# Top-32 attention: the masks of the kept keys come from ScalarE's Sign instead of a VectorE compare, and their count from row sums

## The chip, the core and the metric

The kernel runs on one core of one Trainium2 chip. The metric is the device time of one launch in microseconds. A core has TensorE (PE) for matmuls and transposes, VectorE (DVE), ScalarE (ACT), GpSimd (POOL), and SyncE (SP), which here issues most DMAs. Each engine works through a queue of its own in order, and semaphores tie the queues together.

## The reference, cut to what matters

A model of four residual blocks over x of 4 batches x 512 rows x 256: a 16-head cross-attention, a top-2 mixture of eight experts, the block below, and a 16-head self-attention with gated values. The change touches only the attention in the third block:

```python
Q = (x_text @ Wq).reshape(Bb, Tt, H, DH)            # 4 heads of 32
K = (x_vision @ Wk).reshape(Bb, Gg, H, DH)          # 1601 keys
scores = jnp.einsum('bthd,bghd->bhtg', Q, K) / np.sqrt(DH)
scores = jnp.where(vision_mask[:, None, None, :], scores, -jnp.inf)
topv, topi = jax.lax.top_k(scores, 32)
probs = jax.nn.softmax(topv, axis=-1)
attn = jnp.zeros_like(scores).at[bi, hi, ti, topi].set(probs)
attn_mean = attn.mean(axis=1)                       # over the heads
c_t = jnp.einsum('btg,bgd->btd', attn_mean, x_vision @ Wv)
```

So each query row keeps exactly the 32 largest of its 1601 scores, takes a softmax over those, and the heads' sparse rows are averaged.

## The kernel before, in words

The program runs the first block for all four batches, then the experts, then, batch by batch, the third and the fourth block. In the third, the top-32 attention of a batch is cut into 16 items: item n is tile t = n // 4 of 128 query rows and head h = n % 4. An item is a matrix of 128 rows by 1601 keys. The order of the work is written out by hand in each engine's queue; nothing is planned by a tool. Semaphore counts are per batch, which is what the helper `nth` adds.

The steps of item n and their lines:

- PE, `scores(n)` (L1483 to L1491): four column groups into PSUM banks 0 to 3, each a matmul of queries and keys (L1489) and one of the mask row (L1490). It waits until ScalarE has evicted the scores of n-1, as there is one set of banks.
- ScalarE, `score_out(n)` (L1013): evicts 1601 columns to one of four buffers in SBUF.
- VectorE, `search(n, k)` (L2239): the eight largest of each of 27 parts of 60 columns, as 216 candidates. It is spread over the steps of item n-1. Then four maxima (L2254) and three replacements (L2256) over the 216 give the 32 largest candidates.
- VectorE: the negated maximum (L2265, `top_ready`), then the mask `kept01`: 1 where the score is at least the 32nd candidate (L2269, `choice_ready`), in bf16, double buffered.
- ScalarE: Exp of the whole row (L1048), Exp of the 32 with their sum (L1051).
- PE, `count(n)` (L1493 to L1502): 13 matmuls of a column of ones with the mask, which leave column counts; ScalarE copies these with a row sum into one number (L1050, `count_ready`).
- VectorE, `settle(n-1)` (L2200 to L2219), in the middle of item n: reads that number. If it is not 128 x 32, some row had more than 32 kept (nine of its 32 in one part, or a tie), and an exact search over 1601 columns is run. Then `weight` (L2221 to L2227) takes one over the sum (`w1_ready`).
- GpSimd: multiplies probabilities and mask (L802), and later adds the head to the mean of its tile (L796). ScalarE scales in between (`scale_head`, L1033). The last two heads of a batch are multiplied and added by VectorE (L2278, L2281).
- PE: once per tile, transposes of the mean (L1511) and two blocks of 26 matmuls with the values (L1519, `context`), interleaved with the items; ScalarE evicts the transposes (`attn_turned`, L834 and L830) and the result (L1017).

PE's queue in the loop (L1529 to L1543) is: scores(n+2); for n % 4 = 2 from 6 on 12 transposes; for n % 4 = 0 from 8 on a context block; count(n); for n % 4 = 3 from 7 on a context block; for n % 4 = 2 a wait for the count's copy and the 13th transpose. ScalarE's (L1041 to L1058) is: eviction of n+2, Exp(n), the count's copy, the small Exp, scaling of n-1, and for n % 4 = 2 the evictions of the transposes.

Of the kernel before, what the change touches and what calls it, by code (L numbers as in the profile page):

```python
# [8 lines left out]
BF16 = mybir.dt.bfloat16  # L9
# [6 lines left out]
P = 128  # L16
# [21 lines left out]
H1, D1, TOPK = 4, 32, 32  # L38
ALL_DECIDED = int(np.float32(P * TOPK).view(np.int32))
DROPPED = -3.4e38  # L40
# [28 lines left out]
def program(nc, a, dbg=None):  # L69
    ctx = ExitStack()  # L70
    with ctx:
        def sb(name, shape, dt=F32):
            return ctx.enter_context(nc.sbuf_tensor("sb_" + name, shape, dt))
# [56 lines left out]
        ones_row = sb("ones_row", [1, P], BF16)  # L130
        ones_col = sb("ones_col", [P, 1], BF16)
        norms = sb("norms", [P, 4])
# [108 lines left out]
        kept01 = at(o, [2, KS], BF16); o += KS  # L241
        kept_by_col = at(o, [P]); o += P
        probs1 = at(o, [3, KS]); o += 3 * KS
# [200 lines left out]
        sum1_ready = sem("sum1_ready", 16)  # L444
        choice_ready = sem("choice_ready", 16)
        count_ready = sem("count_ready", 16)
# [249 lines left out]
        def _(pool):  # L696
# [79 lines left out]
            for b in range(NBATCH):  # L776
# [21 lines left out]
                for n in range(TILES * H1 - 2):  # L798
                    e = probs1[:, n % 3, 0:GKEYS]
                    pool.wait_ge(e1_ready, nth(b, e1_ready, n + 1))  # L800
                    pool.wait_ge(w1_ready, nth(b, w1_ready, n + 1))
                    G.tensor_tensor(e, e, kept01[:, n % 2, 0:GKEYS], ALU.mult).then_inc(p1_kept, 1)  # L802
                    if n >= 1:
                        add_head(n - 1)
# [33 lines left out]
        def _(act):  # L838
# [154 lines left out]
            for b in range(NBATCH):  # L993
# [32 lines left out]
                def scale_head(n):  # L1026
                    t = n // H1
                    act.wait_ge(p1_kept, nth(b, p1_kept, n + 1))
                    act.wait_ge(w1_ready, nth(b, w1_ready, n + 1))
                    if n % H1 == 0 and t >= 2:  # L1030
                        act.wait_ge(aT_done, nth(b, aT_done, 4 * (t - 1)))
                    p = probs1[:, n % 3, 0:GKEYS]
                    A(p if n % H1 else p_mean[:, t % 2, 0:GKEYS], p, ACT.Copy, scale=stat1[:, n % 3, WEIGHT:WEIGHT + 1]).then_inc(p1_scaled, 1)  # L1033

# [6 lines left out]
                for n in range(TILES * H1):  # L1041
# [3 lines left out]
                    if n >= 3:  # L1045
                        probs_used(n - 3)
                    bias = stat1[:, n % 3, NEG:NEG + 1]
                    A(probs1[:, n % 3, 0:GKEYS], s_sb[n % 4][:, 0:GKEYS], ACT.Exp, bias=bias).then_inc(e1_ready, 1)  # L1048
                    act.wait_ge(count_done, nth(b, count_done, n + 1))
                    A(kept_by_col[0:1, :], ps[0:1, 7, 3 * P:4 * P], ACT.Copy, accum_out=kept[0:1, n:n + 1]).then_inc(count_ready, 1)  # L1050
                    A(top_e[:, n % 2, :], top[:, n % 2, :], ACT.Exp, bias=bias,  # L1051
                      accum_out=stat1[:, n % 3, SUM:SUM + 1]).then_inc(sum1_ready, 1)
                    if 1 <= n < TILES * H1 - 1:
                        scale_head(n - 1)
# [55 lines left out]
        def _(pe):  # L1110
# [344 lines left out]
            for b in range(NBATCH):  # L1455
# [37 lines left out]
                def count(n):  # L1493

                    pe.wait_ge(choice_ready, nth(b, choice_ready, n + 1))
                    if n >= 1:
                        pe.wait_ge(count_ready, nth(b, count_ready, n))
                    for i in range(KCH):
                        k = -i % KCH
                        ins = mm(ps[0:1, 7, 3 * P:3 * P + KW[k]], ones_col[:, :], kept01[:, n % 2, k * P:k * P + KW[k]],  # L1500
                                 start=(i == 0), stop=(i == KCH - 1))
                    ins.then_inc(count_done, 1)  # L1502
# [171 lines left out]
        def _(dve):  # L1674
# [4 lines left out]
            def setup_program():  # L1679
# [16 lines left out]
                link(V.memset(ones_row[:, :], 1.0))  # L1696
                link(V.memset(ones_col[:, :], 1.0))
                link(V.memset(every[:, :], 1.0))
# [492 lines left out]
            for b in range(NBATCH):  # L2191
# [53 lines left out]
                for n in range(NH):  # L2245
# [17 lines left out]
                    if n >= 3:  # L2263
                        dve.wait_ge(p1_scaled, nth(b, p1_scaled, n - 2))
                    V.tensor_scalar(st[:, NEG:NEG + 1], eights[:, 0:1], -1.0, None, ALU.mult).then_inc(top_ready, 1)  # L2265
                    if n >= 2:
                        dve.wait_ge(p1_kept, nth(b, p1_kept, n - 1))

                    V.tensor_scalar(kept01[:, n % 2, 0:GKEYS], s, eights[:, TOPK - 1:TOPK], None, ALU.is_ge).then_inc(choice_ready, 1)  # L2269

                mean = p_mean[:, (TILES - 1) % 2, 0:GKEYS]
                for n in (NH - 2, NH - 1):
                    if n == NH - 1:
                        settle(n)
                        weight(n)
                    dve.wait_ge(w1_ready, nth(b, w1_ready, n + 1))
                    dve.wait_ge(e1_ready, nth(b, e1_ready, n + 1))
                    link(V.scalar_tensor_tensor(s_cut[:, 0:GKEYS], kept01[:, n % 2, 0:GKEYS], stat1[:, n % 3, WEIGHT:WEIGHT + 1],  # L2278
                                                probs1[:, n % 3, 0:GKEYS], ALU.mult, ALU.mult))
                    dve.wait_ge(p1_added, nth(b, p1_added, n - TILES))  # L2280
                    V.tensor_tensor(mean, mean, s_cut[:, 0:GKEYS], ALU.add).then_inc(p1_added, 1)  # L2281
                dve.wait_ge(p1_added, nth(b, p1_added, TILES * (H1 - 1)))
# [193 lines left out]
```

## Time and profile before

| | us |
|---|---|
| median of 3 runs | 3291.48 |
| lowest and highest | 3287.58, 3298.54 |
| the profiled execution's own time | 3297.39 |
| its span in the profile | 3295.5 |

The span runs from the first to the last instruction of the profiled execution; its own time is that and 1.9 us around it. Granted clock is the share of TensorE's full rate (2.4 GHz) that it was given, in steps of 0.5 and 1; over a stretch it is a mean.

### The profile page before, as it was taken

To read this page: it belongs to the slowest core of one execution; us is meant where nothing else is said; L and a number is where in the kernel's file an instruction comes from. 1 tells how busy PE (TensorE), PEld (TensorE's weight loads), DVE (VectorE), ACT (ScalarE), POOL (GpSimd) and SP (SyncE) were. 2 spreads that over 40 slices of the span, in tenths; PEclk is the share of its full clock that TensorE was granted. 3 is DMA by queue.
4 is the path that set the end of the run, shared out by engine and by line. 5 is a ranking of instruction groups with operands and counts; after the bars stand their busy time and mean duration, and the time that the engine had idled before them with its cause. 6 is when DMAs were issued, how large, how long until landed. Compare 5 with 4: busy or idle time off the path is not lost.

```text
span 3295.5 us, 36665 instructions
## 1 busy us (share of the span) xinstructions
PE 2666.0 (81%) x12668; PEld 1520.5 (46%) x12668; DVE 1837.7 (56%) x4565; ACT 1446.3 (44%) x2310; POOL 1020.1 (31%) x423
## 2 busy tenths in 40 slices
PE   0565889899948996888898878898879798888899
PEld 0522222232225653465574356475356476346467
DVE  8455012121131114865894875795775796685777
ACT  3033567677811222632453541453551354451354
POOL 1023000000011113630751640571460590260292
PEclk9987898999969996889998889998889898789999
DMA  1054842533141111020001011000002000002000
GB/s 55 0 186 156 119 58 53 82 48 44 63 167 41 45 41 39 1 76 25 20 1 39 1 57 43 21 1 14 26 7 93 20 1 7 26 1 93 0 1 7
DMA packets 88476, 146.54 MB, mean 44 GB/s; under 512 B 16724, under 2 KB 58840, under 8 KB 88248
## 3 DMA queue, kind: packets, MB, share of 16 engines
q1 hardware_dynamic: 80760, 134.57, 15.7%
q0 software_dynamic: 7504, 9.35, 1.5%
q8 instruction: 108, 1.77, 0.2%
q14 instruction: 104, 0.85, 0.1%
HBM read 121.17 MB, written 22.88 MB: 44 GB/s over the span
## 4 chain that ended last, share of the span: by engine, by line
PE 61%; DVE 20%; ACT 7%; issue 7%; DMA 3%; SPq 1%; POOL 1%; DVEq 0%; ACTq 0%; POOLq 0%
PE ps L1489 7%; PE ps L1649 6%; PE ps L1640 6%; PE ps L1256 4%; PE ps L1267 4%; PE ps L1519 3%; PE ps L1627 3%; ACT sb_arena L918 3%; PE ps L1424 2%; PE ps L1589 2%; PE ps L1490 2%; DVE sb_arena L2239 2%; PE ps L1443 2%; PE ps L1437 2%; PE ps L1569 2%
## 5 line engine op out<-in xcount | busy, mean ns | idle before, releaser
L918 ACT ACTIVATE sb_arena<-ps 128x1024 f32<-128x1024 f32 x416 | 402.8, 1021 | 177.8 <-PE ps L1256 170.9
L2239 DVE MAX8 sb_arena<-sb_arena 128x8 f32<-128x60 f32 (+1 forms) x1728 | 247.6, 206 | 175.3 <-ACT sb_arena L1013 175.1
L1489 PE MATMUL ps<-sb_arena 128*128 128x512 f32 (+1 forms) x512 | 296.4, 666 | 25.3 <-ACT sb_arena L1013 13.3
L1256 PE MATMUL ps<-sb_arena 96*128 96x512 bf16 x832 | 241.6, 398 | 56.2 <-issue 37.7
L1649 PE MATMUL ps<-sb_arena 128*128 128x512 f32 x512 | 279.4, 630 | 2.7 <-ACT sb_arena L1087 2.7
L688 POOL TENSOR_TENSOR sb_arena<-sb_arena 128x1024 f32<-128x1024 f32 x96 | 223.7, 2330 | 164.8 <-DVEq L2347 153.9
L802 POOL TENSOR_TENSOR sb_arena<-sb_arena 128x1601 f32<-128x1601 f32 x56 | 173.9, 3105 | 314.8 <-DVE sb_arena L2227 314.8
L1640 PE MATMUL ps<-sb_arena 128*128 128x64 f32 x2048 | 260.9, 271 | 0.0
L1640 PEld LDWEIGHTS ps<-sb_arena 128*128 128x128 f32 x2048 | 252.9, 194 | 0.3
L1100 ACT ACTIVATE sb_arena<-ps,sb_arena 128x512 f32<-128x512 f32 x256 | 175.6, 686 | 170.8 <-DVE sb_arena L2388 167.6
L690 POOL TENSOR_TENSOR sb_arena<-sb_arena 128x1024 f32<-128x1024 f32 x84 | 229.9, 2737 | 6.6
L1267 PE MATMUL ps<-sb_arena 128*32 128x512 f32 x1664 | 227.7, 620 | 1.5 <-ACT sb_arena L918 1.5
L2388 DVE TENSOR_REDUCE sb_arena<-ps 128x1 f32<-128x512 f32 x256 | 171.4, 685 | 88.3 <-PE ps L1649 87.8
L737 POOL DMA_INDIRECT taken_rows<-sb_taken,sb_slots x32 | 31.3, 979 | 605.2 <-DVEq L2007 596.6
L1627 PEld LDWEIGHTS ps<-sb_ident,sb_arena 128*128 128x128 f32 x1024 | 130.2, 144 | 189.0 <-issue 125.6
L1013 ACT ACTIVATE sb_arena<-ps 128x1601 f32<-128x1601 f32 x64 | 96.4, 1507 | 248.9 <-PE ps L1490 248.9
L1094 ACT ACTIVATE sb_arena<-ps 128x512 f32<-128x512 f32 x256 | 152.4, 595 | 119.6 <-PE ps L1627 117.1
L1627 PE MATMUL ps<-sb_ident,sb_arena 128*128 128x128 f32 x1024 | 158.3, 278 | 52.4 <-ACT sb_arena L1100 52.4
L1256 PEld LDWEIGHTS ps<-sb_arena 96*128 96x128 bf16 x832 | 58.7, 99 | 271.0 <-ACT sb_arena L918 204.3
L796 POOL TENSOR_TENSOR sb_arena<-sb_arena 128x1601 f32<-128x1601 f32 x40 | 156.6, 3916 | 18.8 <-ACT sb_arena L1033 18.8
L2382 DVE TENSOR_TENSOR sb_arena<-sb_arena,sb_xtn 128x2048 f32<-128x2048 f32 x56 | 149.4, 2667 | 0.1
L1500 PE MATMUL ps<-sb_arena,sb_ones_col 128*1 128x128 bf16 (+1 forms) x832 | 71.8, 253 | 93.7 <-DVE sb_arena L2269 59.8
(343 smaller groups left out, 4798.8 us busy)
## 6 DMA issues: line engine op xcount, KB each, us to landing
sb_arena<-in_ctxT SPq DMA_DIRECT2D x13, 1601.0 KB, 7.4
sb_arena<-k_spill SPq DMA_DIRECT2D x96, 208.0 KB, 8.1
sb_arena<-in_dft SPq DMA_DIRECT2D x5, 2048.0 KB, 7.9
k_spill<-sb_arena SPq DMA_DIRECT2D x12, 832.0 KB, 5.2
sb_arena<-in_w SPq DMA_DIRECT2D x16, 512.0 KB, 6.5
sb_arena<-in_idft SPq DMA_DIRECT2D x4, 2048.0 KB, 9.6
sb_arena<-in_wf SPq DMA_DIRECT2D x8, 1024.0 KB, 13.0
sb_arena<-q_spill SPq DMA_DIRECT2D x96, 64.0 KB, 9.2
```

The source lines that it names most:

```text
L688: link(eng.tensor_tensor(heads(tmp if e else v2[:, :, hs]), src, mix, ALU.mult))
L690: link(eng.tensor_tensor(v2[:, :, hs], v2[:, :, hs], tmp, ALU.add))
L802: G.tensor_tensor(e, e, kept01[:, n % 2, 0:GKEYS], ALU.mult).then_inc(p1_kept, 1)
L918: A(probs0[:, 2 * (m % 4):2 * (m % 4) + 2, :], ps[:, 2 * (m % 2):2 * (m % 2) + 2, :], ACT.Exp).then_inc(pair_probs, 1)
L1100: A(p2[:, n % 4, :], ps[:, S2_BANKS[n % 4], :], ACT.Exp, bias=nmax2[:, t, h:h + 1], accum_out=sums2[:, t, h:h + 1]).then_inc(p2_ready, 1)
L1256: ins = mm(ps[:, 2 * (m % 2) + i, :], k_stack[0:NSPLIT, h, k * P:(k + 1) * P], q_stack[0:NSPLIT, h, :], start=True, stop=True)
L1267: ins = mm(ps[32 * j:32 * j + 32, 4 + q % 2, :], v0s[b % 2][:, k, h * V0W:(h + 1) * V0W], probs0[:, (4 * g + j) % 8, :], start=(k == 0), s ...
L1489: mm(ps[:, j, 0:w], q1z[:, h, t * P:(t + 1) * P], kT1[:, c0:c0 + w], start=True, stop=False)
L1627: ins = tr(ps[:, 2 + n % 2, j * P:(j + 1) * P], p2[:, n % 4, j * P:(j + 1) * P], ident[:, :])
L1640: ins = mm(ps[:, 4 + h % 2, t * D2:(t + 1) * D2], pT2[:, n % 2, j * P:(j + 1) * P], v2[:, j, h * D2:(h + 1) * D2], start=(j == 0), stop=(j ...
L1649: mm(ps[:, S2_BANKS[n % 4], :], q2z[:, h, t * P:(t + 1) * P], kT2[:, h // 2, :], start=True, stop=True).then_inc(s2_done, 1)
L2239: ins = V.max(cand[:, n % 2, 8 * j:8 * j + 8], s_sb[n % 4][:, c0:c0 + w])
```

## The change

The compare L2269 goes. VectorE now makes, beside the negated maximum, a bias per row that is minus the 32nd candidate, moved by 2^-22 of its size so that the candidate itself comes out positive; `top_ready` is raised only behind it. ScalarE takes Sign of score plus bias over the 1601 columns, which gives +1 or -1 in `kept01`, with the row's sum beside it; this is put between the two Exps. PE adds the 128 row sums with one matmul of one column, and ScalarE copies that one number, negated, behind the small Exp. If each row keeps 32, it is 128 x (1601 - 64). Since a dropped key now has -1 where it had 0, the scaling copy becomes Relu, and VectorE's last two products take max(mask, 0) first and the weight in the addition. GpSimd waits for the Sign. `kept01` has two buffers as before; the row sums and the biases have two as well, and ScalarE waits for count and product of n-2 where VectorE waited for the product.

```diff
-ALL_DECIDED = int(np.float32(P * TOPK).view(np.int32))
+ALL_DECIDED = int(np.float32(P * (GKEYS - 2 * TOPK)).view(np.int32))
+JUST_UNDER = 2.0 ** -22
...
-        kept_by_col = at(o, [P]); o += P
+        signs = at(o, [2, 1]); o += 2
+        under = at(o, [2, 2]); o += 4
+        o += P - 6
...
                     pool.wait_ge(e1_ready, nth(b, e1_ready, n + 1))
+                    pool.wait_ge(sign_ready, nth(b, sign_ready, n + 1))
                     pool.wait_ge(w1_ready, nth(b, w1_ready, n + 1))
...
-                    A(p if n % H1 else p_mean[:, t % 2, 0:GKEYS], p, ACT.Copy, scale=stat1[:, n % 3, WEIGHT:WEIGHT + 1]).then_inc(p1_scaled, 1)
+                    A(p if n % H1 else p_mean[:, t % 2, 0:GKEYS], p, ACT.Relu, scale=stat1[:, n % 3, WEIGHT:WEIGHT + 1]).then_inc(p1_scaled, 1)
...
                     A(probs1[:, n % 3, 0:GKEYS], s_sb[n % 4][:, 0:GKEYS], ACT.Exp, bias=bias).then_inc(e1_ready, 1)
-                    act.wait_ge(count_done, nth(b, count_done, n + 1))
-                    A(kept_by_col[0:1, :], ps[0:1, 7, 3 * P:4 * P], ACT.Copy, accum_out=kept[0:1, n:n + 1]).then_inc(count_ready, 1)
+                    if n >= 2:
+                        act.wait_ge(count_done, nth(b, count_done, n - 1))
+                        act.wait_ge(p1_kept, nth(b, p1_kept, n - 1))
+                    A(kept01[:, n % 2, 0:GKEYS], s_sb[n % 4][:, 0:GKEYS], ACT.Sign, bias=under[:, n % 2, 1:2], accum_out=signs[:, n % 2, :]).then_inc(sign_ready, 1)
                     A(top_e[:, n % 2, :], top[:, n % 2, :], ACT.Exp, bias=bias,
                       accum_out=stat1[:, n % 3, SUM:SUM + 1]).then_inc(sum1_ready, 1)
+                    act.wait_ge(count_done, nth(b, count_done, n + 1))
+                    A(kept[0:1, n:n + 1], ps[0:1, 7, 3 * P:3 * P + 1], ACT.Copy, scale=-1.0).then_inc(count_ready, 1)
...
-                    pe.wait_ge(choice_ready, nth(b, choice_ready, n + 1))
+                    pe.wait_ge(sign_ready, nth(b, sign_ready, n + 1))
                     if n >= 1:
                         pe.wait_ge(count_ready, nth(b, count_ready, n))
-                    for i in range(KCH):
-                        k = -i % KCH
-                        ins = mm(ps[0:1, 7, 3 * P:3 * P + KW[k]], ones_col[:, :], kept01[:, n % 2, k * P:k * P + KW[k]],
-                                 start=(i == 0), stop=(i == KCH - 1))
+                    ins = mm(ps[0:1, 7, 3 * P:3 * P + 1], signs[:, n % 2, :], ones[:, :], start=True, stop=True)
                     ins.then_inc(count_done, 1)
...
-                link(V.memset(ones_col[:, :], 1.0))
...
-                    V.tensor_scalar(st[:, NEG:NEG + 1], eights[:, 0:1], -1.0, None, ALU.mult).then_inc(top_ready, 1)
                     if n >= 2:
-                        dve.wait_ge(p1_kept, nth(b, p1_kept, n - 1))
-
-                    V.tensor_scalar(kept01[:, n % 2, 0:GKEYS], s, eights[:, TOPK - 1:TOPK], None, ALU.is_ge).then_inc(choice_ready, 1)
+                        dve.wait_ge(sign_ready, nth(b, sign_ready, n - 1))
+                    low_of, just = under[:, n % 2, 0:1], under[:, n % 2, 1:2]
+                    V.tensor_scalar(st[:, NEG:NEG + 1], eights[:, 0:1], -1.0, None, ALU.mult)
+                    link(V.tensor_scalar(low_of, eights[:, TOPK - 1:TOPK], JUST_UNDER - 1.0, 1.0e-30, ALU.mult, ALU.add))
+                    V.scalar_tensor_tensor(just, eights[:, TOPK - 1:TOPK], -1.0 - JUST_UNDER, low_of, ALU.mult, ALU.max).then_inc(top_ready, 1)
...
-                    link(V.scalar_tensor_tensor(s_cut[:, 0:GKEYS], kept01[:, n % 2, 0:GKEYS], stat1[:, n % 3, WEIGHT:WEIGHT + 1],
-                                                probs1[:, n % 3, 0:GKEYS], ALU.mult, ALU.mult))
+                    link(V.scalar_tensor_tensor(s_cut[:, 0:GKEYS], kept01[:, n % 2, 0:GKEYS], 0.0, probs1[:, n % 3, 0:GKEYS], ALU.max, ALU.mult))
                     dve.wait_ge(p1_added, nth(b, p1_added, n - TILES))
-                    V.tensor_tensor(mean, mean, s_cut[:, 0:GKEYS], ALU.add).then_inc(p1_added, 1)
+                    V.scalar_tensor_tensor(mean, s_cut[:, 0:GKEYS], stat1[:, n % 3, WEIGHT:WEIGHT + 1], mean, ALU.mult, ALU.add).then_inc(p1_added, 1)
```

## Rows read from the trace of the kernel before

**Rows 1.** The page, part 1: busy time, share of the span, instructions

```profile
PE 2666.0 (81%) x12668; PEld 1520.5 (46%) x12668; DVE 1837.7 (56%) x4565; ACT 1446.3 (44%) x2310; POOL 1020.1 (31%) x423
```

**Rows 2.** Busy time by stretch: window, length, PE, PEld, DVE, ACT, POOL, clock, DMA, GB/s

```profile
1297.00:1454.20 157.20, 128.54 (x624) 71.54 (x622) 125.38 (x593) 85.71 (x130) 89.37 (x28) 0.79 0.04 9
```

**Rows 3.** L1013, items 2 to 15, one row per batch: ns, first and last start

```profile
L1013 ACT ACTIVATE sb_arena<-ps x14: 1505/1507/1513, 1297.0 to 1419.3; 128x1601 f32<-128x1601 f32 x14
L1013 ACT ACTIVATE sb_arena<-ps x14: 1505/1507/1513, 1809.1 to 1927.9; 128x1601 f32<-128x1601 f32 x14
L1013 ACT ACTIVATE sb_arena<-ps x14: 1505/1507/1511, 2318.7 to 2437.1; 128x1601 f32<-128x1601 f32 x14
L1013 ACT ACTIVATE sb_arena<-ps x14: 1505/1507/1510, 2836.2 to 2955.1; 128x1601 f32<-128x1601 f32 x14
```

**Rows 4.** Timeline of one period, batch 0: start us, us, engine, line, operation, [idle before]

```profile
1382.09 1.96 DVE L2269 TENSOR_SCALAR sb_arena<-sb_arena 128x1601 bf16<-128x1601 f32 x1
...
1383.03 1.51 ACT L1013 ACTIVATE sb_arena<-ps 128x1601 f32<-128x1601 f32 x1 [2.17 <-PE ps L1490]
...
1384.10 0.86 PE L1500 MATMUL ps<-sb_arena,sb_ones_col 128*1 128x128 bf16 x13 [1.12 <-DVE sb_arena L2269]
1384.43 1.62 ACT L1048 ACTIVATE sb_arena<-sb_arena 128x1601 f32<-128x1601 f32 x1
...
1384.89 1.12 PE L1489 MATMUL ps<-sb_arena 128*128 128x512 f32 x2
1385.95 0.25 ACT L1050 ACTIVATE sb_arena<-ps 1x128 f32<-1x128 f32 x1
...
1386.11 0.18 ACT L1050 ACTIVATION_READ_ACCUMULATOR sb_arena<-ps 1x1 f32 x1
...
1386.50 1.61 ACT L1033 ACTIVATE sb_arena<-sb_arena 128x1601 f32<-128x1601 f32 x1
...
1387.87 0.16 DVE L2225 RECIPROCAL sb_arena<-sb_arena 128x1 f32<-128x1 f32 x1
...
1389.62 1.51 ACT L1013 ACTIVATE sb_arena<-ps 128x1601 f32<-128x1601 f32 x1 [1.50 <-PE ps L1490]
1390.29 0.14 DVE L2265 TENSOR_SCALAR sb_arena<-sb_arena 128x1 f32<-128x1 f32 x1
```

**Rows 5.** Groups by line, 1297 to 1419.3 (batch 0): busy us, mean ns, idle before

```profile
L802 POOL TENSOR_TENSOR sb_arena<-sb_arena 128x1601 f32<-128x1601 f32 x13 | 40.4, 3111 | 79.7 <-DVE sb_arena L2227 79.7
L796 POOL TENSOR_TENSOR sb_arena<-sb_arena 128x1601 f32<-128x1601 f32 x8 | 32.4, 4047 | 0.0
L2269 DVE TENSOR_SCALAR sb_arena<-sb_arena 128x1601 bf16<-128x1601 f32 x13 | 26.7, 2051 | 0.0
...
L1048 ACT ACT_TABLE_LOAD x1 | 1.3, 1283 | 0.0
```

**Rows 6.** Timeline of PE in batch 1, count(1)

```profile
1819.14 1.49 PE L1500 MATMUL ps<-sb_arena,sb_ones_col 128*1 128x128 bf16 x13 [3.80 <-DVE sb_arena L2269]
```

**Rows 7.** Busy time by stretch (columns of rows 2): idle stretch, scores(4), undisturbed scores

```profile
1308.50:1317.00 8.50, 8.50 (x15) 2.50 (x15) 6.59 (x33) 2.19 (x6) 3.02 (x1) 0.50 0.00 0
...
1820.60:1827.40 6.80, 6.80 (x16) 2.04 (x16) 6.57 (x32) 2.19 (x5) 3.02 (x1) 0.67 0.00 0
2325.00:2330.20 5.20, 1.43 (x14) 1.22 (x14) 5.20 (x26) 3.14 (x2) 2.86 (x1) 0.68 0.00 0
2330.20:2338.10 7.90, 7.90 (x15) 2.25 (x15) 6.59 (x33) 2.19 (x5) 3.02 (x1) 0.56 0.01 3
...
1378.37:1383.03 4.66, 4.62 (x12) 1.48 (x12) 4.27 (x25) 2.45 (x7) 2.85 (x1) 1.00 0.00 0
```

**Rows 8.** The chain in order of time, batch 0: start us, us, two context blocks

```profile
1374.48 3.10 PE ps L1519 x26
...
1401.59 4.73 PE ps L1519 x26
```

**Rows 9.** Timeline of VectorE in the tail of batch 0: the weight of item 15

```profile
1440.03 0.21 DVE L2227 TENSOR_SCALAR sb_arena<-sb_arena,sb_tmask 128x1 f32<-128x1 f32 x1
```

More of the change, by code:

```diff
@@ L130, in program @@
         ones_row = sb("ones_row", [1, P], BF16)
-        ones_col = sb("ones_col", [P, 1], BF16)
         norms = sb("norms", [P, 4])
@@ L444, in program @@
         sum1_ready = sem("sum1_ready", 16)
-        choice_ready = sem("choice_ready", 16)
+        sign_ready = sem("sign_ready", 16)
         count_ready = sem("count_ready", 16)
```

## The prediction

> A measurement of this kernel can tell about 0.3% (10 us) from no change.
>
> **What bounds the kernel now.** I read the page first. TensorE is busy 81% of the span, VectorE 56%, ScalarE 44% [rows 1]. That average says little here: the edit touches one stage, the top-32 attention, which runs once in each of four batches. In the first it lasts 157 us, PE works 82% of that at a granted clock of 0.79, VectorE 80% [rows 2]; the other three are alike, so one row stands. So no engine fills the stage; it turns on who waits for whom.
>
> The score eviction (L1013) runs once per item, and its first and last start mark the loop. From that of item 2 to that of item 15 there are 13 periods: 122.3, 118.8, 118.4 and 118.9 us in the four batches, mean 119.6, or 9.2 us a period [rows 3]. These 13 are the ones I have to re-price: in PE's queue the count of item n stands between the scores of item n+2 and those of n+3, for n = 0 to 12.
>
> The timeline of one period shows the order [rows 4]. PE ends its scores, ScalarE evicts them at 1383.03, VectorE ends the compare (L2269, 1382.09 + 1.96 us) at 1384.05, PE starts the 13 count matmuls at 1384.10 and only behind them, at 1384.89, the next scores, which end 4.7 us later: ScalarE evicts again at 1389.62. The compare runs beside the eviction, so PE stood still for only 1.1 us. ScalarE's own work (Exp at 1384.43, two small ones, scaling at 1386.50) lies beside PE's scores and costs nothing. Where VectorE is late, the period is its own: from the compare at 1382.09 to the next L2265 at 1390.29 it is 8.2 us, of which the compare is 2.
>
> **The change, part by part.**
>
> *VectorE loses the compare* (2.05 us a mean of 13 [rows 5]) and gains two one-column operations with one semaphore link; the present one-column L2265 takes 0.14 us [rows 4], so two linked ones are 0.28 at least; I take 0.35. VectorE's loop falls by 1.7 us an item. Whether that arrives depends on the next part.
>
> *ScalarE gains Sign over 1601 columns with a row sum.* It has the shape, source and bias form of the Exp of L1048. Exp's successor starts 1.52 us after it (1384.43 to 1385.95), and the row-sum read that follows the small Copy takes 0.18 [rows 4]; so Sign with its sum is 1.71 us. Bounds: 1.52, and 1.62 + 0.25 = 1.9.
>
> *The wait moves, and this decides.* ScalarE's queue holds the eviction of n+2, Exp(n), Sign(n). PE's holds scores(n+2), count(n), scores(n+3). Count(n) now waits for Sign(n), which stands behind the eviction of scores(n+2). So a closed loop arises: eviction, Exp, Sign, count, next scores, next eviction. Nothing in it overlaps. From eviction to Exp 1.40 us (1383.03 to 1384.43), Exp 1.52, Sign 1.71: 4.63 [rows 4]. The handoff and the one-column matmul in place of 13: the compare-to-count handoff is 0.05, the matmul itself between 0.06 (a thirteenth of the 0.79 us from 1384.10 to 1384.89) and that 0.79, if one costs what the thirteen did; I take 0.15 in all, near the low end, since one column moves in place of 1601. The high end would add 0.7 a period, 36 us in all. Then scores(n+3). PE starts scores 4.8 us after the eviction started, where it was 1.9 in rows 4.
>
> At the full clock scores take 4.7 us, so a plain period is 4.8 + 4.7 = 9.5 us. VectorE is then hidden: from the end of an eviction (1384.54) to L2265 it needs 5.75 us, in which it stands at the count's result after some 2.9 [rows 4]. Now that result comes 4.63 + 0.15 + 0.5 = 5.3 us after the eviction's start, that is 0.9 us late; its loop ends at 1.5 + 5.75 + 0.9 + 0.35 = 8.5 us, and Exp(n+1) is not due before 9.5 + 1.4. The saved compare therefore buys nothing. GpSimd's 3.1 + 4.0 us an item [rows 5] fit in 9.5 as well. ScalarE's sum: 4.63, small Exp and Copy 0.75, scaling 1.6, and in every fourth item the turned probabilities (four evictions of about a third of L1013's 1.51 each, 2.0), together 9.0: hidden. Its new waits for count(n-2) and the product n-2 are for work done a period earlier, and the two waits moved behind Sign are for things ScalarE needs next anyway. GpSimd's added wait for Sign stands ahead of a wait for the weight, which VectorE gives out later: free.
>
> *The clock.* PE's idle stretch grows from 1 or 2 us to 4.6. The trace has a place with just such a stretch: in each batch PE idles 3.8 us before count(1) (batch 1, up to 1819.14 [rows 6]), in the 5.2 us between scores(3) and scores(4). In all four batches the granted clock falls in it (means of 0.68 to 0.80; one of the four rows stands), and scores(4) takes 8.5, 6.8, 7.9 and (batch 3, like the first) 8.5 us at 0.50 to 0.67 instead of 4.66 at 1.00 [rows 7]: 7.9 in the mean, 8.5 when all of it runs at the 1.2 GHz level. A plain period becomes 4.8 + 7.9 = 12.7 us.
>
> *The 13 periods of a batch:*
> - n = 0: 12.7 and a table load of 1.28 [rows 5] that is on the loop now: 14.0.
> - n = 1, 2, 3, 4, 5, 9: plain, 6 x 12.7 = 76.2.
> - n = 6, 10: PE waits for the kept count and turns one last chunk before scores. That count is out at 5.3, the transposes (0.4, for 0.3 and a handoff) at 5.7, so scores start 0.9 later than in a plain one: 2 x 13.6 = 27.2.
> - n = 7, 11: 26 context matmuls stand between count and scores: 3.1 us at full clock, 4.73 where most of it fell in a low stretch [rows 8]. After the idle stretch I take 4.7, and scores behind it at the full clock again, as after the block of rows 8, where the clock had come back: 2 x (4.8 + 4.7 + 4.7) = 28.4.
> - n = 8, 12: the context block (3.1) fills most of the idle stretch, 1.6 us remain: between 9.5 and 12.7, nearer the first as rows 4 kept the clock across 1.1 us; 2 x 10.5 = 21.0.
>
> Sum 166.8 against 119.6: +47.2 a batch, +189 us over four.
>
> *The tail* behind the eviction of item 15: VectorE drops two compares, but Exp(15) and Sign(15) queue on ScalarE behind the turned probabilities of item 14. Today the last weight comes 20.7 us after the eviction (1419.3 [rows 3] to 1440.03 [rows 9]). With the change: top(14) at 7.5, Exp and Sign to 10.8, the small ones to 11.3, scaling and turned chunks to 14.8, Exp(15) and Sign(15) to 18.1, count, copy and weight to 20.0. I take 0. Everything else (Relu for Copy, max for mult in L2278, add in L2281, a memset of one column less at setup) has the same shape as before: 0.
>
> *Tables.* Copy and Exp alternate all through the stage and the trace has one table load there [rows 5]; for Sign no row speaks, bounds 0 and 2 x 1.28 a period. The Trainium skill (ScalarE: Activation LUTs, "Table sets: the hidden batching unit") says cheap functions are in every set as filler, and by that it is 0; no run here shows it yet. The same page ("Rules for kernel authors") sends simple element work to VectorE, up to about three times faster in bf16; by that Sign would be 5.9 us and the sum some 220 us higher, an estimate. The trace disagrees for this shape with an fp32 source: compare 1.96, an activation of 1601 columns 1.62.
>
> The sum stands on the profiled execution, 3297.4 us (span 3295.5), 5.9 above the median 3291.5 and inside the runs shown. Against the median: 3291.5 + 189 = **3480 us**, +5.7%.
>
> **The rivals.**
> 1. *The clock holds.* PE's gaps cost only themselves: 10.8 + 6 x 9.5 + 2 x 10.4 + 2 x 12.6 + 2 x 9.5 = 132.8 a batch, +13.2, +53 in all: 3344. Against it: four falls out of four at an idle stretch shorter than the new one.
> 2. *The clock stays low through the stage:* scores 8.5, context 6.2 (twice 3.1): 14.6 + 6 x 13.3 + 2 x 14.2 + 2 x 19.5 + 2 x 14.9 = 191.6, +72 a batch: 3579. For it: scores(4) was wholly low twice. Against: rows 8 show a context block lifting it again.
> 3. *Faster.* VectorE's loop is the bound in most periods (8.2 us) and its 1.7 us arrive: 13 x 1.7 x 4 = 88, some 5 more in the tail: 3198. This decides as soon as the loop through Sign is shorter than VectorE's; that needs it under 8.2, and it is 9.5 at best, unless scores(n+3) don't stand behind count(n), which the code says they do.
> 4. *Sign needs a table of its own:* 13 x 2.57 x 4 = +134 on top, 3614.
> 5. *The masks miss exactly 32.* The bias is the 32nd value widened by 2^-22 of itself; a neighbour that close sends an item into the exact search (L2206 to L2219), of which the trace has none. Four maxima and four replacements over 1601 columns and two more such passes are some 20 us (ten passes at the compare's 1.96). One or two items: +20 to +40, inside my range; all 64, if Sign is not exact: +1280.
>
> **How the numbers follow.** My forecast, mixed clock, 0.76; rival 1 0.08, rival 2 0.09, rival 3 0.04, rivals 4 and 5 together 0.02; 0.01 that it nets out. The range leaves out rival 1 and the far cases and takes in most of rival 2: 3375 to 3575. Faster 0.04, same 0.01, slower 0.95.
>
> **What would show it.** In the changed profile the chain of waits should alternate ScalarE (eviction, Exp, Sign) and PE (scores) in the stage, and PE's count should wait on Sign in all 64 items. Eviction to eviction should be 9.5 to 13.3 us, first to last some 167 a batch. VectorE should idle at the count's result and be under 65% busy; the stage's clock should be below 0.75. One table load per batch at the Exp. I am wrong if PE starts scores within 3 us of the eviction's start, or if the periods are under 9 us.

## The result, and the profile after

The changed kernel takes 3513.6 us (median of 4, 3512.7 to 3517.3) against 3290.7 for the kernel before on the same chip: ratio 1.068, 95% interval 1.066 to 1.070. It is slower by 6.8%. I had forecast 3480, between 3375 and 3575.

The page of the changed kernel, part 1, and the group of the new count in part 5 (busy us, mean ns, idle before and what ended most of it):

```profile
PE 2709.6 (77%) x11964; PEld 1506.0 (43%) x11964; DVE 1801.1 (51%) x4643; ACT 1541.2 (44%) x2374; POOL 996.8 (28%) x423
...
L1505 PE MATMUL ps<-sb_ones,sb_arena 128*1 128x1 f32 x128 | 12.1, 163 | 295.1 <-ACT sb_arena L1055 227.0
```

VectorE has 37 us less to do than in [rows 1], ScalarE 95 more. PE has 700 instructions fewer and yet is busy for 44 us longer; the granted clock of the whole execution fell from 0.897 to 0.849. And ahead of the count (L1505) PE now stands still for 295 us, 227 of them ended by Sign (L1055).

The eviction's first and last start in each batch, the rows that answer to [rows 3] (L1016 here is L1013 before):

```profile
L1016 ACT ACTIVATE sb_arena<-ps x14: 1505/1507/1509, 1294.9 to 1464.6; 128x1601 f32<-128x1601 f32 x14
L1016 ACT ACTIVATE sb_arena<-ps x14: 1505/1507/1508, 1855.9 to 2027.8; 128x1601 f32<-128x1601 f32 x14
L1016 ACT ACTIVATE sb_arena<-ps x14: 1505/1507/1508, 2424.6 to 2594.4; 128x1601 f32<-128x1601 f32 x14
L1016 ACT ACTIVATE sb_arena<-ps x14: 1505/1507/1511, 2991.2 to 3171.1; 128x1601 f32<-128x1601 f32 x14
```

The 13 periods take 169.7, 171.9, 169.8 and 179.9 us, 691 in all against 478: +213. The tail of a batch, from its last eviction to the first matmul behind its context blocks (L1564, L1560 before), was 35.7 us in the mean of the four and is now 40.0: +17. Everything else together differs by -10 us, in stages that the change does not touch; these take between 2644 and 2675 us in the fourteen profiles of this case, so that -10 says nothing. That makes the 220 us between the two spans.

One plain period of the changed kernel in the timeline, with the steps of [rows 4]:

```profile
1320.44 1.51 ACT L1016 ACTIVATE sb_arena<-ps 128x1601 f32<-128x1601 f32 x1 [4.90 <-PE ps L1497]
1321.84 1.62 ACT L1051 ACTIVATE sb_arena<-sb_arena 128x1601 f32<-128x1601 f32 x1
1323.36 1.62 ACT L1055 ACTIVATE sb_arena<-sb_arena 128x1601 bf16<-128x1601 f32 x1
1324.88 0.19 ACT L1055 ACTIVATION_READ_ACCUMULATOR sb_arena<-sb_arena 128x1 f32 x1
...
1325.12 0.19 PE L1505 MATMUL ps<-sb_ones,sb_arena 128*1 128x1 f32 x2 [4.72 <-ACT sb_arena L1055]
...
1325.24 2.08 PE L1496 MATMUL ps<-sb_arena 128*128 128x512 f32 x2
...
1326.37 0.16 DVE L2228 RECIPROCAL sb_arena<-sb_arena 128x1 f32<-128x1 f32 x1 [1.19 <-ACT sb_arena L1059]
...
1332.92 1.50 ACT L1016 ACTIVATE sb_arena<-ps 128x1601 f32<-128x1601 f32 x1 [5.87 <-PE ps L1497]
```

Read it as one loop: eviction 1320.44, Exp 1.40 later, Sign 1.52 after that, its row sum out at 1325.07, count at 1325.12, scores at 1325.24, next eviction at 1332.92. PE starts scores 4.80 us after the eviction started; the forecast said 4.8. The next scores then took 7.7 us, not 4.7. The reason is in the view of busy time by stretch over the 13 periods of batch 0 (columns as in rows 2):

```profile
1294.90:1464.60 169.70, 116.67 (x312) 49.64 (x312) 92.83 (x546) 89.64 (x115) 69.33 (x22) 0.64 0.01 5
```

The granted clock is 0.64 there; PE is busy 69% of the time, VectorE 55%.

### The profile page after: what moved, and what is told of

It is laid out like the page before. It is cut to its first block, busy times and chain, and to the rows that moved or that the text cites. A ratio compares the mean times of both kernels' runs of the same rounds, so it can differ in the third digit from the quotient of the medians.

```text
span 3515.6 us, 35470 instructions
## 1 busy us (share of the span) xinstructions
PE 2709.6 (77%) x11964; PEld 1506.0 (43%) x11964; DVE 1801.1 (51%) x4643; ACT 1541.2 (44%) x2374; POOL 996.8 (28%) x423
## 4 chain that ended last, share of the span: by engine, by line
PE 60%; DVE 15%; issue 10%; ACT 10%; DMA 2%; SPq 1%; POOL 1%; another core or an unknown queue 1%; DVEq 0%; ACTq 0%; POOLq 0%; PEldq 0%
PE ps L1496 10%; PE ps L1653 6%; PE ps L1644 6%; PE ps L1263 4%; PE ps L1274 4%; PE ps L1631 3%; PE ps L1523 3%; ACT sb_arena L921 3%; PE ps L1497 3%; ACT sb_arena L1055 2%; ACT sb_arena L1051 2%; PE ps L1431 2%; PE ps L1593 2%; PE ps L1450 2%; PE ps L1444 2%
## 5 line engine op out<-in xcount | busy, mean ns | idle before, releaser
L1496 PE MATMUL ps<-sb_arena 128*128 128x512 f32 (+1 forms) x512 | 366.3, 810 | 18.3 <-ACT sb_arena L1008 10.1
L805 POOL TENSOR_TENSOR sb_arena<-sb_arena 128x1601 f32<-128x1601 f32 x56 | 173.8, 3104 | 560.9 <-DVE sb_arena L2230 560.9
L1016 ACT ACTIVATE sb_arena<-ps 128x1601 f32<-128x1601 f32 x64 | 96.4, 1507 | 397.0 <-PE ps L1497 397.0
L1644 PEld LDWEIGHTS ps<-sb_arena 128*128 128x128 f32 x2048 | 252.2, 194 | 0.3
L1505 PE MATMUL ps<-sb_ones,sb_arena 128*1 128x1 f32 x128 | 12.1, 163 | 295.1 <-ACT sb_arena L1055 227.0
L1496 PEld LDWEIGHTS ps<-sb_arena 128*128 128x128 f32 x512 | 109.1, 265 | 95.4 <-issue 67.2
## 6 DMA issues: line engine op xcount, KB each, us to landing
sb_arena<-in_wf SPq DMA_DIRECT2D x8, 1024.0 KB, 13.3
```

Of the source, the lines that this page charges most:

```text
L1496: mm(ps[:, j, 0:w], q1z[:, h, t * P:(t + 1) * P], kT1[:, c0:c0 + w], start=True, stop=False)
L1644: ins = mm(ps[:, 4 + h % 2, t * D2:(t + 1) * D2], pT2[:, n % 2, j * P:(j + 1) * P], v2[:, j, h * D2:(h + 1) * D2], start=(j == 0), stop=(j ...
```

## The experiments

The theory: the loop through ScalarE sets the period (A), PE's longer idle stretch lowers its clock (B). Rivals: ScalarE's added work as such, or the clock alone. Each experiment starts from the changed kernel unless it says otherwise, and its ratio is against the kernel before, run beside it on the same chip. "Less" is against the changed kernel's 3513.6 us, which was measured at another time: the kernel before took 3290.7 us then and between 3279 and 3286 beside the experiments, so a difference of some 12 us in the times alone shows nothing, and there the ratios and the traces decide. A plain period is one with neither transposes nor a context block in it (n = 1 to 5 and 9).

**e1: the count behind the next scores.**

```diff
+                    if n % H1 == 3 and n > H1:
+                        pe.wait_ge(aT_ready, nth(b, aT_ready, 4 * (n // H1)))
+                    elif n >= 1:
+                        count(n - 1)
                     if n % H1 == 2 and n > H1:
                         turn_probs(n // H1 - 1, range(KCH - 1))
+                        count(n)
...
-                    if n % H1 == 3 and n > H1:
-                        pe.wait_ge(aT_ready, nth(b, aT_ready, 4 * (n // H1)))
-                    count(n)
...
+                count(TILES * H1 - 1)
```

> The changed kernel with one thing moved in TensorE's queue: count(n) stands behind scores(n+3) and no longer ahead of it (not for n % 4 = 2 from 6 on, where the transposes need it first). All computation is kept. My theory, the loop eviction, Exp, Sign, count, next scores: without it in 11 of 13 periods, scores start 1.6 us after the eviction started instead of 4.8. The copy of the count on ScalarE now waits for the end of scores, so the period is about 1.6 + 4.7 + 0.3 + scaling 1.6 = 8.2 to 9 us at full clock; the 13 periods fall from 170 to between 110 and 130 us a batch, and the time to between 3280 and 3360. Rival A, ScalarE's added work is the cost (1.7 us more busy time an item wherever it stands): the periods stay near 13 us and the time within 30 us of 3514. Rival B, the lower clock alone is the cost and PE's order has no part: no change either.

Measured: 3421.6 us, ratio 1.042 (1.038 to 1.045), 92 us less than the changed kernel; the 13 periods of batch 0 fall from 170 to 145 us. So the order in PE's queue is part of the loss, and ScalarE's work as such is not what costs. But the time is above the range that I gave. The timeline shows why:

```profile
1320.56 0.19 PE L1505 MATMUL ps<-sb_ones,sb_arena 128*1 128x1 f32 x2
1320.79 0.16 ACT L1059 ACTIVATE sb_arena<-ps 1x1 f32<-1x1 f32 x1 [3.02 <-PE ps L1505]
1320.86 1.63 ACT L1036 ACTIVATE sb_arena<-sb_arena 128x1601 f32<-128x1601 f32 x1
...
1322.39 1.48 ACT L1016 ACTIVATE sb_arena<-ps 128x1601 f32<-128x1601 f32 x1
...
1323.93 2.08 PE L1496 MATMUL ps<-sb_arena 128*128 128x512 f32 x2 [3.18 <-ACT sb_arena L1016]
```

The loop was not cut, it was replaced: ScalarE waits 3.0 us for the count behind the scores, then copies, then scales, and only then evicts. PE idles 3.2 us, these scores run at a clock of 0.50, and the period is 8.5 + 1.8 + 1.5 = 11.8 us, as in four of the 13 of batch 0.

**e2: Sign ahead of Exp on ScalarE.** The block with Sign and its two waits stands ahead of the big Exp and of the wait for its buffer; the same instructions run.

```diff
+                    if n >= 2:
+                        act.wait_ge(count_done, nth(b, count_done, n - 1))
+                        act.wait_ge(p1_kept, nth(b, p1_kept, n - 1))
+                    A(kept01[...], s_sb[n % 4][:, 0:GKEYS], ACT.Sign, bias=under[...], accum_out=signs[...]).then_inc(sign_ready, 1)
...
                     A(probs1[...], s_sb[n % 4][:, 0:GKEYS], ACT.Exp, bias=bias).then_inc(e1_ready, 1)
-                    if n >= 2:
-                        act.wait_ge(count_done, nth(b, count_done, n - 1))
-                        act.wait_ge(p1_kept, nth(b, p1_kept, n - 1))
-                    A(kept01[...], s_sb[n % 4][:, 0:GKEYS], ACT.Sign, bias=under[...], accum_out=signs[...]).then_inc(sign_ready, 1)
```

> The changed kernel with Sign ahead of the big Exp in ScalarE's queue; the same instructions on every engine, all computation kept. My theory: Exp (1.52 us) leaves the loop, PE's scores start 3.3 us after the eviction's start instead of 4.8, and each of the 13 periods of a batch is shorter by 1.5 us at an equal clock, by more where the clock falls less: 80 to 140 us less, 3375 to 3435. Rival A, ScalarE's work as such: no change, as it does the same. Rival B, clock alone: no change unless the clock changes.

Measured: 3413.2, ratio 1.039 (1.035 to 1.042), 100 us less. In the trace PE starts scores 3.3 us behind the eviction's start in every plain period (L1051 is Sign here):

```profile
1317.53 1.51 ACT L1016 ACTIVATE sb_arena<-ps 128x1601 f32<-128x1601 f32 x1 [5.29 <-PE ps L1497]
...
1320.69 0.19 PE L1505 MATMUL ps<-sb_ones,sb_arena 128*1 128x1 f32 x2 [3.20 <-ACT sb_arena L1051]
...
1320.81 2.08 PE L1496 MATMUL ps<-sb_arena 128*128 128x512 f32 x2
```

Two activations that change places, with the same work on every engine, are worth 100 us. The 52 periods sum to 594 us instead of 691. Of these 97 us, 1.5 x 52 = 78 are the shorter loop. The rest is mostly the clock: the scores of n = 8 and 12 take 4.7 us where they took 7.5 in the changed kernel (batch 0). So e2 moves the clock too, and does not keep A and B apart; e3 does that from the other side.

**e3: the same loop, PE kept working.** Ten extra matmuls ("fills"), whose result nobody reads, stand ahead of the count.

```diff
                 def count(n):
+                    if n % H1 != 2 or n < H1:
+                        for _ in range(0 if n % H1 == 0 and n > H1 else 10):
+                            mm(ps[:, 5, 0:P], ident[:, :], ident[:, :], start=True, stop=True)
```

> The changed kernel with ten extra matmuls of 128 columns (2.1 us at full clock, their result is not used) in PE's idle stretch ahead of the count, where no transposes or context block stand there already; nothing of the computation is left out. It separates the idle stretch from the clock. My theory: the start of scores stays 4.8 us behind the eviction, the granted clock rises where the fill is enough, and scores fall from 7.7 us towards 4.7; the plain periods go from 12 towards 9.5 us, and the time falls by 60 to 130 us, to 3385 to 3455. If the clock has no part in the loss: no change or a few us more. If the clock is all of it (PE's order has no part): back to the kernel before, 3291.

Measured: 3450.2, ratio 1.050 (1.047 to 1.054), 63 us less, inside the range near its upper end. By stretch, batches 0 and 1:

```profile
1302.60:1458.80 156.20, 130.61 (x493) 68.13 (x493) 92.84 (x546) 89.56 (x114) 69.41 (x22) 0.77 0.01 5
1850.00:2000.00 150.00, 120.85 (x494) 64.43 (x494) 92.59 (x546) 89.61 (x115) 66.52 (x22) 0.84 0.02 6
```

The clock is 0.77 and 0.84 instead of 0.64, scores still start 4.8 us behind the eviction, and several plain periods are 9.5 us, the full-clock figure of the forecast. So B is a cost of its own: PE does more and the kernel is faster. The 52 periods give 61 us of it, the tails 11.

**e4: the bias without scalar_tensor_tensor.**

```diff
-                    V.scalar_tensor_tensor(just, eights[:, TOPK - 1:TOPK], -1.0 - JUST_UNDER, low_of, ALU.mult, ALU.max).then_inc(top_ready, 1)
+                    V.tensor_scalar(just, eights[:, TOPK - 1:TOPK], -1.0 - JUST_UNDER, low_of, ALU.mult, ALU.max).then_inc(top_ready, 1)
```

> The changed kernel with the bias's second operation as tensor_scalar with a pointer for the second constant instead of scalar_tensor_tensor; the same values. In the changed profile the one-column scalar_tensor_tensor takes 0.85 to 2.3 us and ends with GpSimd's product or sum of the moment. Theory: it waits for a port that GpSimd holds, and the other form does not, so it takes 0.15 us; in the loop nothing comes of it (VectorE is not on it), in the tail of a batch Exp(14) and Exp(15) start 0.8 and 2.2 us earlier: 8 to 14 us less in all. Rival: the operation itself is slow whatever its form: no change.

Measured: 3510.6, ratio 1.068 (1.064 to 1.072): in the time no difference from the changed kernel can be told. The operation takes 214 ns in all 64 places where it took 1068 in the mean:

```profile
L2273 DVE TENSOR_SCALAR sb_arena<-sb_arena x64: 212/214/216, 1282.6 to 3182.0; 128x1 f32<-128x1 f32 x64
```

The tail is 37.1 us in every batch instead of 40.0, which is the 12 us expected, so the theory of the operation is shown and the time is not. In this profile 7 of the 12 are lost again in the 13 periods of batch 3, 186.9 us instead of 179.9, at a clock of 0.60 instead of 0.66.

**f1: e1, with ScalarE's scaling ahead of the count's copy, VectorE's read of it two steps later, and e4's bias.**

```diff
-                    act.wait_ge(count_done, nth(b, count_done, n + 1))
-                    A(kept[0:1, n:n + 1], ps[0:1, 7, 3 * P:3 * P + 1], ACT.Copy, scale=-1.0).then_inc(count_ready, 1)
                     if 1 <= n < TILES * H1 - 1:
                         scale_head(n - 1)
+                    act.wait_ge(count_done, nth(b, count_done, n + 1))
+                    A(kept[0:1, n:n + 1], ps[0:1, 7, 3 * P:3 * P + 1], ACT.Copy, scale=-1.0).then_inc(count_ready, 1)
...
-                        if k == 4 and n >= 1:
+                        if k == 6 and n >= 1:
```

> As e1 (the count behind the next scores), and also: the count's copy on ScalarE behind the scaling of item n-1, VectorE reads the count three steps later (k = 6), and the bias in the tensor_scalar form. All computation is kept. In e1 the copy waited for the end of the low-clock scores and held the scaling and the next eviction back: periods of 11.8 us are scores 8.5 + copy and scaling 1.8 + eviction 1.5. My theory: with the scaling ahead of the copy these fall to 8.5 + 0.3 + 1.5 = 10.3 at the low clock and to VectorE's or ScalarE's 7.5 to 8 at the full one; 13 periods a batch 115 to 130, the time 3270 to 3340. If ScalarE's or VectorE's work were the bound: no gain over e1's 3422.

Measured: 3359.4, ratio 1.025 (1.020 to 1.029). Plain periods are 10.3 us at the low clock, as expected; the time is 20 us over the range (the profiled run, at 3344.5, is the fastest of its four). The 13 periods take 134 us in three batches and 141 in the fourth, which has the exact search of f4 in it, where I had expected 130 at most. The longest are n = 6 and 10, 15.4 and 16.4 us, which keep the old order because the transposes need the count.

**f2: f1 with Sign ahead of Exp.**

> As f1, with Sign ahead of Exp on ScalarE. The loop through Sign is already cut in most periods there; it remains in those of n = 6 and 10, and in what VectorE waits for. Theory: within 20 us of f1, 4 to 15 us less if anything. Rival: Sign first keeps helping as in e2 (100 us): then the loop is not what e1 and f1 cut.

Measured: 3368.2, ratio 1.026 (1.023 to 1.029), no different from f1. The same plain period, first of f1, then of f2:

```profile
1318.57 1.51 ACT L1016 ACTIVATE sb_arena<-ps 128x1601 f32<-128x1601 f32 x1
...
1320.12 2.07 PE L1496 MATMUL ps<-sb_arena 128*128 128x512 f32 x2 [1.66 <-ACT sb_arena L1016]
```

```profile
1319.00 1.50 ACT L1016 ACTIVATE sb_arena<-ps 128x1601 f32<-128x1601 f32 x1
...
1320.55 2.08 PE L1496 MATMUL ps<-sb_arena 128*128 128x512 f32 x2 [1.66 <-ACT sb_arena L1016]
```

In both PE starts scores 1.55 us behind the eviction's start, whichever activation comes first, and n = 2 to 5 of batch 0 take 10.3 us each. What e2 gained by shortening the loop is not to be had where the loop is gone. That is the second half of the proof for A.

**f3: e2, e3 with eight fills, e4.**

> The changed kernel's order on TensorE, with Sign ahead of Exp (e2), eight filling matmuls in the idle stretch (e3) and the tensor_scalar bias (e4). The three effects are of separate causes: loop length 3.3 us, clock, tail. Theory: plain periods 3.3 + 4.7 = 8.0 us where the clock holds, 13 periods 115 to 130 us a batch against 146 in e2 and 157 in e3; time 3300 to 3370. If loop and clock were one and the same cause, the two would not add: about the better of e2 and e3, 3413.

Measured: 3312.4, ratio 1.009 (1.006 to 1.012). The 13 periods of batch 0 are 123.6 us, plain ones 8.0 = 3.3 + 4.7 but for n = 1 (10.4). e2 alone gave 100 us, e3 alone 63; together with e4 they give 201. So the causes add, and are not one. In the 52 periods alone the profiles show 179 us against 97 + 61 = 158, somewhat more than the sum. A likely reason, which no run takes apart, is that a shorter idle stretch is easier to fill: 10 of the 13 scores of batch 0 run at the full clock here, 5 of 13 in e3.

```profile
1291.70:1415.30 123.60, 107.20 (x457) 57.85 (x458) 80.95 (x540) 88.21 (x115) 65.06 (x21) 0.89 0.02 7
```

**f4: the widening halved** (JUST_UNDER is 2.0 ** -23).

> The changed kernel with the bias widened by 2^-23 of the 32nd value instead of 2^-22. In the changed profile one item of batch 3 went through the exact search and its period took 28.6 us where its neighbours take 11.5 to 13.3. Theory: a neighbour's score lies within 2^-22 of the 32nd, not within 2^-23: no exact search, the 13 periods of batch 3 near 170 instead of 180 us, the time 5 to 20 us less. Rival: the item has more than 32 equal or has nine of its 32 in one part, whatever the bias: the search stays.

Measured: 3502.2 (2 runs), ratio 1.067 (1.063 to 1.070), which the time alone can't tell from the changed kernel. The trace can. In the changed kernel one item of batch 3 went through the exact search, four maxima over 1601 columns among it; here no such instruction is in the trace, and the 13 periods of batch 3 are 169.8 us instead of 179.9:

```profile
L2215 DVE MAX8 sb_arena<-sb_arena x4: 1829/1830/1831, 3035.2 to 3046.8; 128x8 f32<-128x1601 f32 x4
```

(this row is the changed kernel's; f4 has none to answer to it, nor have g1 and g3, which share its widening, while every other run with 2^-22 has four), and of f4:

```profile
L1016 ACT ACTIVATE sb_arena<-ps x14: 1505/1507/1508, 2987.7 to 3157.5; 128x1601 f32<-128x1601 f32 x14
```

**g1: everything that helped, in the changed kernel** (Sign first, tensor_scalar, 2^-23, fills of 8, and 5 behind transposes, in bank 7 behind the wait for the last count's copy).

> The changed kernel with Sign ahead of Exp, the tensor_scalar bias, the 2^-23 widening, and filling matmuls (8 of 128 columns, 5 behind transposes, none where a context block stands) in PE's idle stretch, now also for n = 6 and 10, which ran at the low clock in f3 (8.3 us of scores). All computation is kept. Theory: f3's 3312, less 18 us for the exact search in batch 3, less up to 3 us in each of n = 6 and 10 of the four batches (0 to 25): 3270 to 3295, about the kernel before. If it lands under the kernel before by more than 0.3%, the move of the compare pays once loop and clock are looked after.

Measured: 3284.1 (12 runs), ratio 1.002 (1.000 to 1.004): the kernel before, no more. With loop, clock, tail and search looked after, the moved compare gains nothing over a kernel before that has no fills; g2 gives that one fills too.

**g2: fills in the kernel before.**

```diff
-                    pe.wait_ge(choice_ready, nth(b, choice_ready, n + 1))
                     if n >= 1:
                         pe.wait_ge(count_ready, nth(b, count_ready, n))
+                    for _ in range(0 if n % H1 == 0 and n > H1 else 5):
+                        mm(ps[:, 7, P:2 * P], ident[:, :], ident[:, :], start=True, stop=True)
+                    pe.wait_ge(choice_ready, nth(b, choice_ready, n + 1))
```

> The kernel before with 5 filling matmuls ahead of each count (1.1 us at full clock), nothing else. In its profile four to six scores a batch ran at the low clock (up to 8.5 us against 4.7), 43 us in all four batches, of which part was hidden. Theory: the fill holds the clock in some of them: 0 to 30 us less, 3255 to 3285. Rival: the fill delays scores by as much as it saves: within 10 us of 3285.

Measured: 3255.8, ratio 0.993 (0.990 to 0.996), faster than the kernel before by 0.7%. In its profile one of the 13 scores of a batch runs at a lowered clock, where the kernel before has three to five. This is the fair match for g1, on the same chip and beside it: with fills on both sides the moved compare costs 28 us (ratios 1.002 and 0.993, intervals apart). So g1 is level with the kernel before only because it has fills and that one has none.

**g3: f1 with the 2^-23 widening and fills beside the eviction.**

> f1 (the count behind the next scores, the copy behind the scaling, VectorE's read later, tensor_scalar bias) with the 2^-23 widening and 7 filling matmuls of 128 columns (1.5 us at full clock) ahead of scores, beside the eviction. In f1 the plain periods were 10.3 us with scores at the low clock. Theory: where the clock holds, they are bound by ScalarE or VectorE, 7.7 to 8.1 us as f1 shows for its full-clock ones; n = 6 and 10 keep their 14 to 16. 13 periods 112 to 126 a batch, the time 3265 to 3320. If the low clock can't be held off there: about f1 less 15, 3345.

Measured: 3303.4, ratio 1.008 (1.005 to 1.011). Plain periods are 7.0 to 7.6 us at the full clock, where the kernel before has 9.8 in the mean of batch 0. But n = 6 and 10 cost 14 to 16 us each (8.1 and 9.1 there) and eat it: the 52 periods sum to 478 us in both kernels. The tail is 38.5 us a batch instead of 35.7, which is 11 us more.

**g4: g2 with 12 fills ahead of count(1).**

> g2 with 12 filling matmuls instead of 5 ahead of count(1), where PE idles longest; all computation is kept. In g2 the scores behind that count still ran at the low clock (6.8 to 8.5 us), the only low ones left of the 13. Theory: the 13 periods of a batch fall from 111.5 to 114.1 to about 108 to 110, the time by 8 to 16 us, to 3240 to 3248. Rival: a single idle stretch before it has already taken the clock down, and the fill, then twice as long, only delays: no gain.

Measured: 3242.7, ratio 0.988 (0.985 to 0.991), the fastest of all. By stretch, the 13 periods of batch 0:

```profile
1290.70:1400.80 110.10, 101.72 (x580) 58.01 (x580) 101.59 (x532) 70.89 (x101) 72.37 (x21) 1.00 0.02 8
```

The clock is 1.00 throughout (0.98 in batches 2 and 3), and these 13 periods take 110 us instead of 122; in the other batches it is 110 or 111 instead of 118 or 119. VectorE and PE are each busy 92% of it. The chain of waits lies on VectorE but for n = 7, 8, 11 and 12, where it lies on PE with the context blocks; so VectorE is the bound of the other periods.

## Why the prediction was right

*The loop.* Right in every step: 1.40 + 1.52 + 1.71 from eviction to row sum, 4.80 us to the scores against 4.8. e2 and f2 together show it: the same swap is worth 100 us with the loop and nothing without it. I had written that PE's count would wait on Sign in all 64 items; the profile names Sign in 52. For the other twelve, n = 7, 11 and 15 of each batch, which wait for the turned probabilities ahead of the count, it names none; n = 7 and 11 count 4.7 us behind the eviction like the rest, n = 15 is in the tail.

*Count and handoff, 0.15.* Measured: 0.05, and 0.12 from the count's start to the scores. Right.

*VectorE is hidden.* Right: it waits 1.19 us for the count's copy (forecast 0.9), and its busy share is 55% (forecast under 65).

*The clock.* Right in kind, and the size of a single row was off to both sides. Plain periods were to be 12.7 us; they alternate between 11.5 and 12.5 in batch 0, five of them and one of 13.3: 72.7 us instead of 76.2. In batch 1 three of the six are 13.3 and the sum is 76.3, so 12.7 was a mean that fits and not what a period does. The stretch's clock is 0.64 (forecast under 0.75). Rival 2, low throughout, is refuted by those 6.6 us scores, rival 1 by all of it.

*The context blocks, the first mis-sized term.* For n = 7 and 11, I took 4.7 us for the block between count and scores and had scores 4.8 us behind the eviction plus that; measured are 10.6 (so 5.8 for the block, which starts at a clock of 0.50) and a period of 15.4 and 15.3, not 14.2. For n = 8 and 12 I took 10.5, since the block fills the idle stretch; measured 12.4, with scores of 7.5 and 7.6 us at 0.57 behind the 1.6 us that remain of it. In batch 3 the same n = 8 took 9.5, with scores at the full clock, so the short stretch does not lower the clock every time. Together +6 in batch 0, and the plain ones -3.5.

*The exact search* of rival 5 happened in one item, where I had set +20: its own period is 28.6 us instead of 12.5, and the 13 of the batch are 10 us longer, as some periods behind it ran at a higher clock (f4).

*The tail, the second mis-sized term.* I took 0; it is +4.3 us a batch. I had given the two new one-column operations 0.35 us together. The second of them takes 0.85 to 2.3 in 60 of 64 items, 1.07 in the mean of all:

```profile
1471.09 3.02 POOL L805 TENSOR_TENSOR sb_arena<-sb_arena 128x1601 f32<-128x1601 f32 x1 [6.43 <-DVE sb_arena L2230]
...
1473.15 0.96 DVE L2273 SCALAR_TENSOR_TENSOR sb_arena<-sb_arena 128x1 f32<-128x1 f32 x1
1474.15 1.63 ACT L1051 ACTIVATE sb_arena<-sb_arena 128x1601 f32<-128x1601 f32 x1 [2.94 <-DVE sb_arena L2273]
...
1479.44 3.02 POOL L798 TENSOR_TENSOR sb_arena<-sb_arena 128x1601 f32<-128x1601 f32 x1 [5.34 <-ACT sb_arena L1036]
1480.16 2.32 DVE L2273 SCALAR_TENSOR_TENSOR sb_arena<-sb_arena 128x1 f32<-128x1 f32 x1
1482.51 1.63 ACT L1051 ACTIVATE sb_arena<-sb_arena 128x1601 f32<-128x1601 f32 x1 [1.53 <-DVE sb_arena L2273]
```

In the loop it has slack; in the tail Exp waits for it. e4 takes 2.9 us a batch away. The rest, 1.4, was not taken apart; the 104 context matmuls of batch 0's tail are busy for 15.0 us instead of 12.9. The tail also gives 2.9 us back in e3, which leaves this operation as it is, so the clock has a part in it.

*Tables.* None was loaded for Sign: had each item loaded two, the loop would be 2.6 us longer than the 4.80 measured. So the Trainium skill's statement (ScalarE: Activation LUTs, "Table sets: the hidden batching unit"), that cheap functions such as relu and copy are in every set, agrees with the trace; the page does not name Sign among them, and the trace has no load between it and Exp.

*The compare.* I wrote that the trace disagrees with the rule that VectorE is the faster for such work, from 1.96 us against 1.62. That was a misreading: about half of the 1.96 is a wait, and alone the compare takes 1.05. The last section has the rows.

In sum, periods +213 (forecast +189), tail +17 (0), the rest -10. The 24 us that the periods missed by are 3, 5 and 3 in batches 0 to 2 and 13 in batch 3, where the exact search is. The mechanism was right. That batches 0 to 2 came within 5 us has luck in it: in batch 0 the context periods are 6 us over and the plain ones 3.5 under.

## What to carry to other kernels

Before moving work to an idle engine, write down the queue of each engine and follow who stands behind whom: an engine that is 44% busy can still close a loop in which nothing overlaps. Price a longer idle stretch of TensorE twice, once as the stretch and once as the clock behind it; filling it with matmuls whose result nobody uses gave 1.2% in the kernel before, where the change lost 6.8%. Give such a repair to both kernels before you compare them: g1 alone looks like no loss, g1 against g2 is 28 us of loss. And a wait that is moved may only be replaced by the next one in the same queue, as in e1: look at the queue again after each cut.

## What the hardware showed that I had not expected

VectorE's one-column scalar_tensor_tensor ends when GpSimd's tensor_tensor ends: 1473.15 + 0.96 is 1474.11, and so is 1471.09 + 3.02; 1480.16 + 2.32 is 1482.48, GpSimd's end 1482.46. It is so in 60 of the 64 items, each within 0.02 us. The other four, the first item of each batch, have no GpSimd work beside them and take 0.16:

```profile
L2273 DVE SCALAR_TENSOR_TENSOR sb_arena<-sb_arena x64: 158/970/2322, 1283.2 to 3186.7; 128x1 f32<-128x1 f32 x64
```

With tensor_scalar and a pointer, the same values take 0.21 with or without GpSimd (e4). The Trainium skill (SBUF — State Buffer, "Who interferes with whom") says that VectorE and GpSimd share a port pair which the first to start holds for its whole instruction, and that a VectorE instruction with two SBUF inputs contends for it; the trace agrees.

It also says this of tensor_scalar in a two-port mode. The trace does not show the mode, but the old compare waits in the same way in the kernel before:

```profile
1380.18 3.02 POOL L802 TENSOR_TENSOR sb_arena<-sb_arena 128x1601 f32<-128x1601 f32 x1 [4.00 <-DVE sb_arena L2227]
...
1382.09 1.96 DVE L2269 TENSOR_SCALAR sb_arena<-sb_arena 128x1601 bf16<-128x1601 f32 x1
...
1432.39 3.02 POOL L796 TENSOR_TENSOR sb_arena<-sb_arena 128x1601 f32<-128x1601 f32 x1 [4.71 <-ACT sb_arena L1033]
1432.65 3.61 DVE L2269 TENSOR_SCALAR sb_arena<-sb_arena 128x1601 bf16<-128x1601 f32 x1
```

GpSimd ends at 1383.20 and the compare 0.85 us later; at 1435.41 and 0.85 later again; and so in 60 of 64 items. The four with no GpSimd work beside them, the first of each batch, are the shortest, 1.05 us:

```profile
L2269 DVE TENSOR_SCALAR sb_arena<-sb_arena x64: 1046/1959/3632, 1285.2 to 2968.5; 128x1601 bf16<-128x1601 f32 x64
```

So the compare is an operation of 1.05 us and, for the rest of its 1.96, a wait for GpSimd. An activation of 1.62 us was no bargain for it. No run here kept the compare and took that wait away, so what it would bring stays open.
